# Graph attention and expert layer: one 96-row product per head for the scores, one projection per quarter turn, row normalisations on ScalarE

## What is computed

```
x   = x + attention(layernorm(x), adj)          # 16 heads of 32, scores * 512**-0.5 + 2 * adj
        p = softmax(q k^T * scale + adj + adj)  # a row whose scores are all 0 gives 0
        o = (p v) Wo^T
x   = x + experts(layernorm(x))                 # 8 experts of 512 x 512, the 2 best per token
        scores = max(x gate_W + gate_b, 1e-4);  p = softmax(scores);  top 2 of 8
        w = max(p, 0.1) / (sum over the 2);  y = sum_e w_e (x W_e + b_e) / 2
```

## Time and profile before

| what | value |
|---|---|
| median of the runs | 1900.24 us |
| the profiled execution | 1902.03 us, span 1900.2 us |
| mean granted clock of TensorE | 0.969 |
| busy share of the span: PE, PEld, DVE, ACT, POOL | 90%, 73%, 71%, 47%, 47% |
| `phase_a`, with its start and tail | up to about 1400 us |
| `phase_b` | from about 1405 us to the end |

### The profile page before, as it was taken

How to read it: one execution, slowest core, us unless ns; L and a number is a source line. 1 busy time by engine, 2 the same in 40 slices (tenths; PEclk the granted TensorE clock), 3 DMA queues, 4 the chain that set the end, 5 groups by cost and what they waited for, 6 DMA issues and landing times. The chain is left out here.

```text
span 1900.2 us, 41822 instructions
## 1 busy us (share of the span) xinstructions
PE 1714.6 (90%) x11600; PEld 1381.2 (73%) x11600; DVE 1347.7 (71%) x4756; ACT 886.5 (47%) x2924; POOL 894.8 (47%) x1468
## 2 busy tenths in 40 slices
PE   4999999999999999999999999999536999999996
PEld 3777777777777777777777777776425778888885
DVE  4668787888888888888888888887543455555554
ACT  2566665656665656566666666665301111111111
POOL 2235444445444444544444544444423456655655
PEclk8999999999999999999999999999758999999998
DMA  6324344334434433433433433433278989888987
GB/s 205 88 66 114 110 115 123 104 104 121 122 101 123 117 99 111 121 115 107 131 104 109 119 118 103 129 93 99 82 266 225 264 177 175 165 164 164 167 158 106
DMA packets 185201, 251.07 MB, mean 132 GB/s; under 512 B 18192, under 2 KB 91920, under 8 KB 184848
## 3 DMA queue, kind: packets, MB, share of 16 engines
q1 hardware_dynamic: 131936, 136.77, 25.7%
q0 software_dynamic: 29680, 69.55, 18.1%
q10 hardware_dynamic: 23360, 42.08, 7.0%
HBM read 105.59 MB, written 109.19 MB: 113 GB/s over the span
## 5 line engine op out<-in xcount | busy, mean ns | idle before, releaser
L561 ACT ACTIVATE prob<-prob,nmax 128x128 f32<-128x128 f32 x1024 | 400.4, 393 | 370.1 <-DVE amax L682 370.1
L942 POOL TENSOR_TENSOR prob<-prob,rinv 128x512 f32<-128x512 f32 x256 | 276.5, 1100 | 237.4 <-DVE rinv L705 236.9
L1142 POOL DMA_INDIRECT out<-yt,token x135 | 212.0, 1571 | 220.1 <-DVE yt L1108 90.5
L678 DVE CUSTOM_DVE_ANT_0 prob<-ps_s,bias 128x128 f32<-128x128 f32 x1024 | 236.5, 286 | 73.0 <-PE ps_s L367 55.5
L1078 ACT ACTIVATE xgT_hi<-ps_x 128x512 fp32r<-128x512 f32 x135 | 80.8, 598 | 415.3 <-PE ps_x L1050 310.0
L1062 PE MATMUL ps_y<-we_hi,xgT_hi 128*128 x540 | 229.0, 424 | 22.0 <-DVE xgT_lo L1097 10.9
L1064 PE MATMUL ps_y<-we_hi,xgT_lo 128*128 x540 | 216.4, 401 | 0.0
L1063 PE MATMUL ps_y<-we_lo,xgT_hi 128*128 x540 | 216.2, 400 | 0.0
L923 POOL TENSOR_SCALAR var<-mv 128x1 f32<-128x1 f32 (+1 forms) x96 | 21.6, 225 | 366.2 <-DVE mv L851 271.4
L561 ACT ACTIVATION_READ_ACCUMULATOR prob<-prob,nmax 128x1 f32 x1024 | 193.5, 189 | 0.0
L616 ACT ACTIVATE pT<-ps_t 128x512 f32<-128x512 f32 x256 | 151.1, 590 | 82.5 <-PE ps_t L436 82.1
(11 more groups left out here) (153 smaller groups left out, 4591.5 us busy)
## 6 DMA issues: line engine op xcount, KB each, us to landing
xg<-x_lists ACTq DMA_DIRECT2D x135, 260.5 KB
kblk<-kT SPq DMA_DIRECT2D x256, 128.0 KB, 2.8
xin<-x SPq DMA_DIRECT2D x64, 256.0 KB, 2.9
xres<-x SPq DMA_DIRECT2D x64, 256.0 KB, 2.6
out<-xres SPq DMA_DIRECT2D x64, 256.0 KB, 2.8
e_stage<-expert_W SPq DMA_DIRECT2D x32, 256.0 KB, 3.9
e_parts<-e_hi SPq DMA_DIRECT2D x32, 256.0 KB, 3.0
e_parts<-e_lo SPq DMA_DIRECT2D x32, 256.0 KB, 3.7
```

The lines of the kernel that those rows point to most:

```text
L561: last = nc.scalar.activation(prob[:, r, c, h, :], prob[:, r, c, h, :], ACT.Exp, bias=nmax[:, r, n:n + 1], scale=-1.0, accum_out=rsum[:, r ...
L678: last = nc.vector.tensor_tensor_reduce(out=prob[:, r, c, h, :], in0=ps_s[c % 2][:, P * h:P * h + P], in1=bias[:, b.ring(4), :], scale=-1. ...
L942: tt(prob[:, r, q], prob[:, r, q], rinv[:, r, HC * q:HC * q + HC].unsqueeze(2).to_broadcast([P, HC, P]), ALU.mult)\
L1142: pool.indirect_dma_start(out=out, out_offset=bass.IndirectOffsetOnAxis(ap=token[:, m, :], axis=0), in_=yt[:, r, :], in_offset=None, compu ...
```

## The change

The loop over turns is written out with plain numbers t and c, from `FIRST = -6` to `LAST = B + 7`, in place of `Item`, `graph`, `pair` and `turns`. In it:

- Scores. q and k are stacked per head in three groups of 32 rows: `qs` holds (q_hi, q_hi, q_lo), `ks` holds (k_hi, k_lo, k_hi). One product over 96 rows gives what the three gave. A quarter has 4 products of 128 columns.
- The stacks are built by DMA: 12 for k and 12 for q per graph, each 32 rows of 2 KB (`stack`). The memory `kblk` and its zeroing are gone. `qT` and `kT` are now kept by graph, so their low parts are made in two halves per unit.
- Units. `big(t, c)` gives exactly one of K, Q, V, O per quarter in bank `ps_p[c % 2]`; `small(t, c)` gives X and X2 in a bank of their own, `ps_m`. The probabilities have one bank `ps_t` instead of two.
- In a quarter TensorE now makes scores, times_v, the turned probabilities, X or X2, and only then the projection. ScalarE copies the turned probabilities before the exponentials, not after.
- ScalarE applies both normalisations (`first_norm`, `second_norm`: Identity with a scale and a bias per row). GpSimd's `rstd` has two instructions more, for the bias -mean * rstd.
- ScalarE copies `ps_o` to the memory tile `oT` and rounds that to `oT_hi`; GpSimd makes `oT_lo`.
- There are four scatter semaphores in place of two, so a tile of `xn2` waits only for the scatter that read this tile.

```diff
-        kblk = sb("kblk", [P, 2, 2 * DC, HC * P], f32r)
+        qs = sb("qs", [3 * HD, 2, HC, DC, P], f32r)
+        ks = sb("ks", [3 * HD, 2, HC, DC, P], f32r)
...
-        QUARTERS = ([[("Q", 0, 1)], [("X2", -3, 0), ("O", -2, 0)], [("K", 2, 0)], [("K", 2, 1)]],
-                    [[("V", 1, 0)], [("X", 3, 0), ("O", -2, 0)], [("X", 3, 1), ("Q", 1, 0)], [("X2", -3, 0), ("V", 1, 1)]])
...
+            kind, n, part = ([("K", p + 1, 0), ("K", p + 1, 1), ("O", t - 2, 0), ("Q", p + 1, 0)],
+                             [("Q", p + 1, 1), ("V", p + 1, 0), ("O", t - 2, 0), ("V", p + 1, 1)])[t % 2][c]
...
+            if t % 2 and c < 2:
+                return ("X", t // 2 + 2, c) if okp(t // 2 + 2) else None
+            if c == 2:
+                return ("X2", t - 3, 0) if ok(t - 3) else None
...
+            def stack(tile, parts, b, done):
+
+                r = b % 2
+                for i, part in enumerate(parts):
+                    for h in range(HC):
+                        sp.dma_start(tile[HD * i:HD * i + HD, r, h, :, :].rearrange("p c t -> p (c t)").bitcast(f32),
+                                     part[HD * h:HD * h + HD, r, :, :].rearrange("p c t -> p (c t)").bitcast(f32)).then_inc(done[r], 16)
+
+            def stack_k(b):
+                hold(k_lo_done, 2 * (b // 2) + 2)
+                if b >= 2:
+                    hold(s_full, 4 * (b - 2) + 4)
+                stack(ks, (kT_hi, kT_lo, kT_hi), b, ks_in)
...
-                three(ps_s[c % 2][:, :], qT_hi[:, c, t], qT_lo[:, c, t], kblk[:, r, c, :], kblk[:, r, DC + c, :], True, True).then_inc(s_full, 1)
+                for h in range(HC):
+                    last = mm(ps_s[c % 2][:, P * h:P * h + P], qs[:, r, h, c, :], ks[:, r, h, c, :], start=True, stop=True)
+                last.then_inc(s_full, 1)
...
+                if kind == "K":
+                    act.wait_ge(K_full, 2 * n + part + 1)
+                    if n >= 1:
+                        for r in range(2):
+                            act.wait_ge(ks_in[r], STACK * n)
...
+            def first_norm(b):
+                k = b % 4
+                act.wait_ge(rstd1_step, RSTD * (b // 2) + RSTD)
+                nc.scalar.activation(xin[:, k, :], xin[:, k, :], ACT.Identity, bias=off1[:, k:k + 1], scale=rstd1[:, k:k + 1]).then_inc(xn_done, 1)
...
+                        nc.scalar.activation(oT[:, :, :].rearrange("p c t -> p (c t)"), ps_o[:, :], ACT.Copy).then_inc(oT_done, 1)
...
+                        nc.scalar.activation(oT_hi[:, :, :], oT[:, :, :], ACT.Copy).then_inc(oT_hi_done, 1)
...
+                for g in range(2):
+                    to, less = (w[:, g, 2 * part:2 * part + 2, :] for w in (lo, hi))
+                    if kind == "K":
+                        last = tt(to, of[:, :, g, :], less.bitcast(f32), ALU.subtract)
...
+                        tt(oT_lo[:, :, :], oT[:, :, :], oT_hi[:, :, :].bitcast(f32), ALU.subtract).then_inc(oT_lo_done, 1)
```

More of the change, by code:

```diff
@@ L235, in number @@
[L235 to L266, removed]
-            return None
@@ L367, in three, with wait_bank @@
                 return mm(out_, lhs_lo, rhs_hi, start=False, stop=last)
[L369 to L372, removed]
-            def work(g, j, n):
-                kind, it, part, count = use(g, j, n)
-                if not it.valid:
-                    return
-                bank = ps_p[bank_of(j, n)]
-                if kind in ("K", "Q"):
-                    pe.wait_ge(xT_lo_done, it.count(2, 2))
-                    if isinstance(g, int) and 2 * g + it.off == 0:
+            def wait_bank(before):
+                if before:
+                    pe.wait_ge(*emptied(before))
@@ L516, in _, with halves, read_projection @@
             matrix_hi(1, "q")
-            def read(g, j, n):
-                kind, it, part, count = use(g, j, n)
-                if not it.valid or kind == "O":
+            def halves(tile, part, bank):
+                return (tile[:, :, 2 * part:2 * part + 2, :].rearrange("p g c t -> p c g t"),
+                        bank[:, :].rearrange("p (c g t) -> p c g t", c=2, g=2))
+            def read_projection(t, c):
+                unit = big(t, c)
+                if not unit or unit[0] == "O":
@@ new lines, in exponentials @@
+            def exponentials(b, c):
+                n, r = DC * b + c, b % 2
+                act.wait_ge(absmax_done, n + 1)
+                if b >= 2 and c == 0:
+                    act.wait_ge(rinv_step, 4 * (b - 2) + 4)
+                for h in range(HC):
+                    i = HC * c + h
+                    last = nc.scalar.activation(prob[:, r, c, h, :], prob[:, r, c, h, :], ACT.Exp, bias=nmax[:, r, i:i + 1],
+                                                scale=-1.0, accum_out=rsum[:, r, i:i + 1])
+                last.then_inc(exp_done, 1)
@@ L980, in _, with second_rstd @@
-            turns(body)
-            for a in range(2):
-                pool.wait_ge(scattered[a], 32 * (B // 2))
+                        hold(step_sem, base + i + 2)
+            def second_rstd(b):
+                k = b % 4
+                hold(mean2, b + 1)
+                if b >= 4:
+                    hold(xn2_done, b - 3)
+                own = slice(k, k + 1)
+                rstd(rstd2_step, RSTD * b, var2[:, own], nwt2[:, own], rstd2[:, own], nmu2[:, own], off2[:, own], mv2[:, k, 0:1], mv2[:, k, 1:2], 1)
@@ L985, in phase_b @@
+            for k in range(4):
+                pool.wait_ge(scattered[k], 32 * (B // 4))
 def phase_b(nc, v):
```

849 lines of the change are left out of this document (423 added, 426 removed).

## The result

The changed kernel takes 1922.33 us (median of 4 runs, 1915.42 to 1925.3), the kernel before 1899.63 on the same chip: a ratio of 1.0115, interval 1.0086 to 1.0144. It is slower by some 22 us, where 1760 was forecast. The profiled execution has 1915.42 us, its span 1913.5.

A forecast was written before the change was run, and what follows sets the result against it. TensorE was taken to bound the first phase, busy 38.96 of 41.03 us a pair. Sum: 1902 - 87 (scores) - 48 (waits) + 2 (start) - 7 (tail) = 1762, less 1.8: 1760 us; range 1725 to 1850.

The forecast's parts named there:

- I take 0.33, the cheapest row: SyncE's queue: issue time in us of each 32-piece stacking DMA; 48 make 16 us, 21 of 36.8 a pair with the rest.
- Slack 1.9 us, so nothing is added: Odd graph's k stack lands at 21.1 us, before ScalarE overwrites K's high part at 23.0; no time added.
- Rival 2: SyncE's queue is late: at 0.64 us a stacking DMA, k lands 1.8 us late, +58, 1818 us; chance 0.12.
- Score products: TensorE's scores: four 128-column products at 0.11 us replace three taking 0.78; 0.34 less per quarter, -87 us over 256.
- Waits of TensorE: Waits for X's input and O's bank: 1.5 of 2.07 us a pair go, -48 us over 32 pairs.
- I count half of this wait as gone: TensorE's wait for X's normalised input, 1.0 us a pair before; ScalarE now makes that input.
- costed at nothing because TensorE covers it: Added work per 36.8 us pair: ScalarE to 29.4 us, VectorE 28.8, GpSimd 23.3; no time added.
- Rivals 1 and 4: Rival 1: 128-column fp32r products slow, 0.27 each, 1924, chance 0.12; rival 4: four products in 0.78 us, 1847, chance 0.03.
- Rival 5: Stacking DMAs are served one after the other, 0.95 us each: 50.6 us a pair, about 2200 us; chance 0.02.
- Rival 3: TensorE's waits only change their names: 2.07 us a pair stay, 1808 us; chance 0.11.
- Start: Kernel start: q's first stack is covered by the two V units; +2 us, once.
- Tail: Kernel end: four scatter semaphores end VectorE's 7.0 us wait in L818 for another tile's scatter; -7 us.

The follow-up runs named there:

- the like-for-like test: Kernel before with 28 more small DMAs a graph on SyncE's queue, the same rows read from on-chip memory (2291.73 us) or from DRAM (1993.08 us).
- the best version of this study: Changed kernel with 9 DMAs a stack, X's normalisations ahead of the exponentials, and a separate semaphore for the DMA copying finished rows: 1772.56 us, ratio 0.9348.
- the ninth DMA: In the changed kernel with 9 DMAs a stack in place of 12 (1830.05 us), the one that copies 32 finished rows to the rows holding the same values.

## Why the prediction was wrong

**SyncE's queue: the step that failed.** It is the sentence "I take 0.33, the cheapest row", and behind it "16 us", "21 of 36.8" and "Slack 1.9 us, so nothing is added". Measured were a median of 0.59 us and, in the pair shown, a mean of 0.68: 32.5 us a pair for the stacks, 9.1 for the rest with its wait, where I had "some 5". So the queue needs 41.6 us and not 21, and the 36.8 us of the forecast cannot be had: (41.57 - 36.8) x 32 = 153 us, by far the most of the miss of 162. I had let the time of an issue grow with its pieces, since `kblk` with 256 pieces took 0.64 and `xres` with 128 took 0.33. The runs show hardly a trace of that: on-chip copies of 32 pieces (2 KB or 64 KB in all) and of 96 (192 KB) take about 0.59, `kblk` with 256 a median of 0.61. What the like-for-like test does show is the side: 0.59 from on-chip memory, 0.42 from DRAM. The nearest row was `kblk`, the only other copy from on-chip memory to on-chip memory, and I took the farther one because it suited the reasoning on pieces. The slack of 1.9 us went with it. In the pair shown, whose even turn opens at 716.9, the odd graph's k took 8.2 us to issue and not 4.0, and it was begun 2.9 us before that turn and not 4.1; K was ready to be copied 4.5 us into it, as forecast (4.6), and the stack came 2.3 us later.

**Rival 2 named the mechanism and still missed the size.** K's high part waits, the copy of turned probabilities behind it, then TensorE: all seen. It priced that at 1.8 us a pair (2.3 in the pair shown; TensorE's own wait 72.4 / 26 = 2.8), with a queue at 36 of 36.8 us. It left out a mean above the median, the 2.3 us a pair in which the queue waits for its own `out` (61.0 of 1100 us in the kernel before, so it was there to read), and TensorE's clock after the wait. Once the queue is longer than the pair, the price is not a lateness but the whole queue. The Trainium skill, Perfetto Trace Analysis, section What "DMA-bound" means, tells a kernel bound on the issuing engine's sequencer from one bound on the DMA engines; the runs agree for the first (the engines stood at 0.57). That section of the Trainium skill advises large descriptors for both; here the same bytes in pieces of the same 2 KB, but a third of the DMAs, gave 1823 us in place of 1922, and an issue with pieces of 64 B took the same 0.59 us as one with pieces of 2 KB.

**Score products: right in kind, 13 us too large.** Taken 0.44 us for four, measured 0.49, that is one every 0.122 us, at the edge of the 0.12 that I had named as the sign of being wrong: 256 x 0.29 = 74 and not 87 us. The new place behind the gate's products takes some 0.09 x 3 x 32 = 9 us of it back. But the term also stood by itself in the sum, and the run with the products alone got none of it.

**Waits of TensorE: right in sum only after a further edit.** O's wait went. X's wait stayed, 1.5 us a pair as soon as the queue was relieved, since ScalarE made the second normalisation behind the exponentials of quarter 3 and the shorter products brought TensorE there sooner. "I count half of this wait as gone" was wrong for the change as written: once the queue was relieved, it grew from 1.0 us a pair to 1.5. With the normalisation moved, TensorE is idle 13.0 of 800 us (400 to 1200), 0.6 a pair, which is what the forecast had left.

**Other engines: the loads nearly right, the order not.** A normalisation took 0.80 to 0.82 (0.83). A pair has 28.1 us of ScalarE (29.4 forecast), 22.7 of GpSimd (23.3) and 30.5 of VectorE (28.8, so 1.7 too few), and the load of none of them set the pair. But "costed at nothing because TensorE covers it" missed ScalarE's order, worth 41 us once the queue was out of the way. Rivals 1 and 4 fell with the 0.49 us. Rival 5 fell as well: a stack's DMAs are issued every 0.6 us and land after 2.0, so they overlap. Rival 3, waits that only change their names, was hidden behind the queue and came true in good part behind it: with the queue relieved, 1.5 of the 2.07 us a pair were back, now as a wait for ScalarE.

**Start: 11 us too small.** The first pair's product came 13.5 us later (178.8; 165.3 before), with 9.6 us of waiting for q's first stack, which I had held to be covered; with a relieved queue and the new order it came at 166.8. **Tail:** from the last such product to the end went 512.5 us before, 504.6 after, yet 512.9 in the run with the old products, which has the same four semaphores, and 505.5 in the run with the new products alone, which has the old two. The -7 is not told apart from such differences.

The way from forecast to result, by differences of runs: 1760, + 13 for the products gives 1773, and the best version of this study takes 1773. From there + 16 for the copy's wait on the ninth DMA (1789), + 41 for the place of the normalisation (1830), + 92 for the queue (1922). The first step is worked out, the others are measured. It is a way through kernels and not a list of causes in the changed one: this has no ninth DMA, so those 16 us belong to the price of relieving its queue by a copy, and as long as its queue is full the place of the normalisation is worth nothing in it. The runs were made on several chips, on which the kernel before took 1894 to 1900 us, so each step is good to some 5 us. That they close to the microsecond is luck, the more so since start and tail are in them.

## What to carry to other kernels

A queue is an engine: sum its issues per round of the loop, at the mean of the row whose two sides are of the same kind, add the waits that it has itself, and compare the sum with the length of the round before saying that anything is hidden. When a change multiplies DMAs, ask first whether the same data can move in fewer, for instance by copying what is already stacked. And a saving on a busy engine is worth what the order around it lets through: the same four products gave 0 us in one order and about 37 in the other.

## What the runs showed of the hardware that I had not expected

A DMA holds SyncE's queue for about as long when it moves 192 KB (medians of 0.52 to 0.61 us) as when it moves 2 KB (0.59), both sides being on the chip; for 32 rows of 8 KB in one piece each it is 0.51. The same 2 KB from DRAM take 0.42, but DMAs with DRAM on one side range from 0.33 to 0.66 in the kernel before. The means are higher, 0.67 and 0.68 in the streams shown.

A 96-row product is no faster than a 128-row one (0.49 and 0.48 us for four).

A gap on TensorE does not always bring its clock down. With one gap of 1.4 us a pair on average, some 3 us at 1.2 GHz came in 5 of 20 pairs, and in 7 of 20 with one of 1.5 us; with gaps of 1.4 and 1.7 us in each pair (the products alone, in the old order) in 9 of 19; with two of about 1.0 to 1.1 us (the kernel before) in 2 of 19; with one of 3 us (the changed kernel) in 16 of 19. In the best version, idle for 6 of 800 us, the clock stayed at 2.4.
